# The tail of a two-layer cross-attention kernel: another order of its last block, one inverse root less, and the last products moved from GpSimd to VectorE

## The chip, the cores and the metric

The kernel runs on one core of a Trainium2 chip. A core has five engines, each with its own instruction stream: TensorE (PE) multiplies matrices and writes to the accumulator memory (`ps`), ScalarE (ACT) applies functions element by element, VectorE (DVE) does element-wise arithmetic and reductions, GpSimd (POOL) does element-wise arithmetic too, and SyncE (SP) issues transfers. Engines wait for each other through semaphores. The metric is the device time of one launch in microseconds (us); lower is better.

## The reference

Input `x` is [2, 1024, 256], the context [2, 77, 256], all float32. Layer 0 is self-attention, cross-attention and a gated feed-forward network, each behind a layer norm and with a residual. Layer 1 is one cross-attention with a single head and an RMS norm at the end. The change touches layer 1 alone:

```python
Q = x @ Wq.T + bq;  K = ctx @ Wk.T + bk;  V = ctx @ Wv.T + bv
attn = softmax(Q @ K.T / sqrt(256), axis=-1)
out  = attn @ V @ Wfc.T + bfc
y    = out + x
return norm_w * (y * rsqrt(mean(y * y, axis=-1) + 1e-8))
```

## The kernel before

The 2048 rows of `x` are 16 tiles of 128 rows, and 4 blocks (`blk` 0 to 3) of 4 tiles (`TPB`); blocks 0 and 1 belong to the first batch element. `x` stays in SBUF, [128, 16, 256], and each step adds its result to it. The order on each engine is written out by hand: the five functions `_(eng)` at the end of `build` are the five instruction streams.

Layer 1's matrices are folded ahead into `g1`, `cb` and `vw`, so that a block needs these steps:

- `turn` and `turn_copy` (X3): `x` is turned by TensorE, and ScalarE copies it to `xT`;
- `l1_scores`: 8 matmuls against `g1`; `l1_max` (VectorE): adds `cb`, takes the row maximum, scales it;
- `l1_exps` (ScalarE): 4 exponentials of 128x77 with their sums;
- `l1_turn` (TensorE): turns the 4 tiles of exponentials; `l1_turn_copy` (ScalarE): copies them to `p1T`;
- `l1_weigh` (TensorE): 4 products with `vw`, one per tile, each written to its own bank; a block's product may overwrite a bank once the residual of the block before has read it (`l_y`);
- `l1_residual` (VectorE): a reciprocal of the sums, then 4 multiply-adds of 128x256 into `x`;
- `l1_squares` (ScalarE): 4 squares of 128x256 with their sums (`l_sq`);
- `l1_root` (VectorE): the inverse root in 12 chained instructions, 3 to start and 3 Newton steps of 3, each of which waits for the one before;
- the end: y times the root times `norm_w`. For blocks 0 to 2 ScalarE multiplies by the root (`l1_scale`) and GpSimd by `norm_w` (line 664, 4 products of 128x256 a block); for block 3 VectorE does both in one instruction (line 1888). SyncE then stores the block (line 569), 512 KB.

The scores of blocks 0 to 2 are made while the feed-forward network still runs; block 3 alone has its scores after it. What follows the network is called the tail here. Its order stands at lines 1198 to 1208 (TensorE), 1459 to 1473 (ScalarE) and 1875 to 1889 (VectorE). Line numbers in the text are those of this kernel.

Of the kernel before, what the change touches and what calls it, by code (L numbers as in the profile page):

```python
# [33 lines left out]
ALU = mybir.AluOpType  # L34
# [3 lines left out]
B, S, D = 2, 1024, 256  # L38
# [4 lines left out]
BLOCKS = T // BLK  # L43
TPB = BLK // P
# [26 lines left out]
RMS_EPS = 1e-8  # L71
# [11 lines left out]
ROW_BO1, ROW_BO2, ROW_BFF2, ROW_W, ROW_BFC = range(5)  # L83


def build(nc, a):
    with ExitStack() as ctx:
        ends, sizes = {}, {}

        def sb(name, shape, dt=F32):  # L90
            t = ctx.enter_context(nc.sbuf_tensor(name, shape, dt))
            ends[name] = nc.sbuf_base
            sizes[name] = int(np.prod(shape[1:])) * mybir.dt.size(dt)
            return t
# [5 lines left out]
        def sem(name):  # L100
            return ctx.enter_context(nc.semaphore(name))

        def scratch(name, shape, dt):
# [10 lines left out]
        x = sb("x", [P, TILES, D])  # L114
# [11 lines left out]
        rows = sb("rows", [P, 5, D])  # L126
# [63 lines left out]
        m1, nm1, sum1, r1, ss1, rms, ms, half_ms = (sb(n, [P, BLOCKS, TPB]) for n in ("m1", "nm1", "sum1", "r1", "ss1", "rms", "ms", "half_ms"))  # L190
# [49 lines left out]
        l_full, l_added, l_max, l_exp, l_turned, l_pT, l_pv, l_y, l_sq, l_root, l_scaled, l_out, l_last = (  # L240
            sem(f"l_{n}") for n in ("full", "added", "max", "exp", "turned", "pT", "pv", "y", "sq", "root", "scaled", "out", "last"))
# [163 lines left out]
        def _(eng):  # L405
# [155 lines left out]


            out_v = a["out"].rearrange("b (t p) d -> p (b t) d", p=P)
            for blk in range(BLOCKS):
                if blk < BLOCKS - 1:
                    eng.wait_ge(l_out, TPB * (blk + 1))
                else:
                    eng.wait_ge(l_last, TPB)
                eng.dma_start(out_v[:, TPB * blk:TPB * blk + TPB, :], x[:, TPB * blk:TPB * blk + TPB, :]).then_inc(y_out, 16)
            eng.wait_ge(y_out, 16 * BLOCKS)  # L570

# [4 lines left out]
        def _(eng):  # L576
# [81 lines left out]
                        eng.tensor_tensor(lo, m.rearrange("p (t n) -> p t n", t=HT), hi, ALU.subtract).then_inc(m_parts, 1)  # L658


            for blk in range(BLOCKS - 1):
                for i in range(TPB * blk, TPB * blk + TPB):
                    eng.wait_ge(l_scaled, i + 1)
                    eng.tensor_tensor(x[:, i, :], x[:, i, :], rows[:, ROW_W, :], ALU.mult).then_inc(l_out, 1)


        @block.tensor
        def _(eng):
# [486 lines left out]
            def l1_turn(blk):  # L1155
                eng.wait_ge(l_exp, TPB * (blk + 1))
                if blk >= 2:
                    eng.wait_ge(l_pT, blk - 1)
                for t in range(TPB):
                    mm_ = eng.transpose(ps[0:CTX, LINEAR + blk % 2, P * t:P * t + P], s1[:, blk, t, :], ident[:, :])  # L1160
                mm_.then_inc(l_turned, 1)

            def l1_weigh(blk):
                eng.wait_ge(l_pT, blk + 1)
                for t in range(TPB):
                    n = TPB * blk + t
                    if blk >= 1:
                        eng.wait_ge(l_y, n - TPB + 1)
                    eng.matmul(ps[:, WIDE[t], 0:D], p1T[0:CTXP, blk, P * t:P * t + P],
                               vw[0:CTXP, blk // 2, :], start=True, stop=True).then_inc(l_pv, 1)  # L1170
# [4 lines left out]
            for n in range(FC * BLOCKS + FF_LAG):  # L1175
# [14 lines left out]
                blk, i = x3_step(n)  # L1190
# [6 lines left out]
            last = BLOCKS - 1  # L1197
# [5 lines left out]
            l1_scores(last)  # L1203
            l1_turn(2)
            l1_weigh(1)
            l1_weigh(2)
            l1_turn(last)
            l1_weigh(last)


# [1 line left out]
        def _(eng):  # L1212
            def turn_copy(phase, blk):

                for c in range(NC):
                    eng.wait_ge(turn_full, 2 * TURNS.index((phase, blk)) + c + 1)
                    src = ps[:, turn_bank(phase, blk, c), :]
                    if phase in (ATT1, ATT2):
                        eng.activation(attT[blk % 2][:, c, :], src, ACT.Copy).then_inc(turn_done, 1)
                    elif phase == X3:  # L1220
                        eng.activation(xT[:, c, BLK * blk:BLK * blk + BLK], src, ACT.Copy).then_inc(turn_done, 1)
                    else:
                        i = COL_LN + 4 * (LN1, LN2, LN3).index(phase)
                        eng.activation(xT[:, c, BLK * blk:BLK * blk + BLK], src, ACT.Identity,
                                       scale=cols[:, i + c:i + c + 1], bias=cols[:, i + 2 + c:i + 3 + c]).then_inc(turn_done, 1)
# [186 lines left out]
            for n in range(FC * BLOCKS):  # L1412
                blk, f = divmod(n, FC)
# [3 lines left out]
                i = COL_FF + FC + f  # L1417
# [10 lines left out]
                done, i = x3_step(n)  # L1428
# [5 lines left out]
            def l1_exps(blk):  # L1434
                eng.wait_ge(l_max, 2 * (blk + 1))
                for t in range(TPB):
                    eng.activation(s1[:, blk, t, :], s1[:, blk, t, :], ACT.Exp, scale=L1_SCALE, bias=nm1[:, blk, t:t + 1],
                                   accum_out=sum1[:, blk, t:t + 1]).then_inc(l_exp, 1)

            def l1_turn_copy(blk):  # L1440
                eng.wait_ge(l_turned, blk + 1)
                eng.activation(p1T[0:CTX, blk, :], ps[0:CTX, LINEAR + blk % 2, :], ACT.Copy).then_inc(l_pT, 1)

            def l1_squares(blk):
                for t in range(TPB):
                    n = TPB * blk + t
                    eng.wait_ge(l_y, n + 1)
                    if n >= 1:
                        eng.wait_ge(l_sq, n)
                    eng.activation(sq[:, :], x[:, n, :], ACT.Square, accum_out=ss1[:, blk, t:t + 1]).then_inc(l_sq, 1)  # L1450

            def l1_scale(blk):
                eng.wait_ge(l_root, blk + 1)
                for t in range(TPB):
                    y = x[:, TPB * blk + t, :]
                    eng.activation(y, y, ACT.Copy, scale=rms[:, blk, t:t + 1]).then_inc(l_scaled, 1)

            last = BLOCKS - 1
# [2 lines left out]
            l1_turn_copy(0)  # L1461
            l1_turn_copy(1)
            turn_copy(X3, last)
            l1_turn_copy(2)
            l1_squares(0)
            l1_exps(last)
            l1_squares(1)
            l1_turn_copy(last)
            l1_scale(0)
            l1_squares(2)  # L1470
            l1_scale(1)
            l1_squares(last)
            l1_scale(2)


        @block.vector
        def _(eng):
# [23 lines left out]
            def root_steps(v, y, w, h, scale, e, ready=None):  # L1501


                for out, ops in ((w, (v, scale, e, ALU.mult, ALU.add)), (h, (w, -0.5, None, ALU.mult)),
                                 (y.bitcast(I32), (w.bitcast(I32), -0.5, float(0x5F3759DF), ALU.mult, ALU.add))):
                    at = begin(eng.tensor_scalar(out, *ops))
                    yield
                    eng.wait_ge(dve_step, at)
                for i in range(3):
                    for in0, in1 in ((y, y), (w, h)):  # L1510
                        at = begin(eng.tensor_tensor(w, in0, in1, ALU.mult))
                        yield
                        eng.wait_ge(dve_step, at)
                    ins = eng.scalar_tensor_tensor(out=y, in0=w, scalar=1.5, in1=y, op0=ALU.add, op1=ALU.mult)
                    if i == 2 and ready is not None:
                        ins.then_inc(ready, 1)
                        return
                    at = begin(ins)
                    yield
                    eng.wait_ge(dve_step, at)  # L1520
# [325 lines left out]
                    eng.scalar_tensor_tensor(out=x[:, n, :], in0=ps[:, WIDE[t], 0:D], scalar=r1[:, blk, t:t + 1],  # L1846
                                             in1=x[:, n, :], op0=ALU.mult, op1=ALU.add).then_inc(l_y, 1)

            def l1_root(blk):
                eng.wait_ge(l_sq, TPB * (blk + 1))  # L1850
                for _ in root_steps(ss1[:, blk, :], rms[:, blk, :], ms[:, blk, :], half_ms[:, blk, :], 1.0 / D, RMS_EPS, l_root):
                    pass

            last_piece, after_cross = after_cross, chain(1, 1)
            for n in range(FC * BLOCKS + FF_LAG):
# [8 lines left out]
                blk, f = divmod(n, FC)  # L1864
                if f == 4 and blk + 1 < BLOCKS:
                    x_low(blk + 1)
                blk, f = divmod(n - FF_LAG, FC)
# [3 lines left out]
                blk, i = x3_step(n)  # L1871
# [3 lines left out]
            last = BLOCKS - 1  # L1875
            l1_residual(0)
            l1_max(last)
            l1_residual(1)
            l1_root(0)
            l1_residual(2)  # L1880
            l1_root(1)
            l1_residual(last)
            l1_root(2)
            l1_root(last)
            eng.wait_ge(l_root, BLOCKS)
            for t in range(TPB):
                y = x[:, TPB * last + t, :]
                eng.scalar_tensor_tensor(out=y, in0=y, scalar=rms[:, last, t:t + 1],
                                         in1=rows[:, ROW_W, :], op0=ALU.mult, op1=ALU.mult).then_inc(l_last, 1)


# ---- launch: one core; the host only lays data out
# [40 lines left out]
```

## Time and profile before

| | |
|---|---|
| median of 3 runs | 755.87 us (753.74, 755.87, 755.88) |
| the profiled execution's own time | 756.13 us |
| its span, first to last instruction | 753.9 us |
| mean granted TensorE clock | 0.949 of full speed |
| last product on VectorE starts | 748.83 us |

The profile is of one execution. Times in its rows are us from the start of the span. A row of the timeline has the start, the duration, the engine, the source line, the operation, what it writes and reads (buffer names without their numbers; the exponentials' array shows as `probs`), the shapes and the count; in brackets the idle time before it and who ended that. A row may merge several instructions of one kind. A matrix product of float32 shows as two MATMUL records.

### The profile page before, as it was taken

To read this page: it belongs to the slowest core of one execution; us is meant where nothing else is said; L and a number is where in the kernel's file an instruction comes from. 1 tells how busy PE (TensorE), PEld (TensorE's weight loads), DVE (VectorE), ACT (ScalarE), POOL (GpSimd) and SP (SyncE) were. 2 spreads that over 40 slices of the span, in tenths; PEclk is the share of its full clock that TensorE was granted. 3 is DMA by queue.
4 is the path that set the end of the run, shared out by engine and by line. 5 is a ranking of instruction groups with operands and counts; after the bars stand their busy time and mean duration, and the time that the engine had idled before them with its cause. 6 is when DMAs were issued, how large, how long until landed. Compare 5 with 4: busy or idle time off the path is not lost.

```text
span 753.9 us, 11161 instructions
## 1 busy us (share of the span) xinstructions
PE 669.6 (89%) x4072; PEld 320.7 (43%) x4072; DVE 538.1 (71%) x929; ACT 488.4 (65%) x853; POOL 99.0 (13%) x152
## 2 busy tenths in 40 slices
PE   4989799999999999999999879679989999999982
PEld 2644122222222222222223335325547878888871
DVE  6678989999999999999974527636853854343367
ACT  2543289999999999999998643446553233233374
POOL 2081800000000000000000100264100110000004
PEclk9999699999999999999999987878998999999995
DMA  9457440202020200000000021111000000000003
GB/s 297 182 190 232 104 181 1 71 1 71 1 72 1 53 19 5 25 2 29 2 1 1 33 78 33 48 56 42 3 1 1 0 1 1 1 1 1 1 0 112
DMA packets 35113, 36.87 MB, mean 49 GB/s; under 512 B 6132, under 2 KB 28276, under 8 KB 34804
## 3 DMA queue, kind: packets, MB, share of 16 engines
q1 hardware_dynamic: 33904, 35.87, 14.9%
q0 software_dynamic: 1024, 0.24, 0.3%
q8 instruction: 32, 0.52, 0.3%
q14 instruction: 21, 0.17, 0.1%
q10 hardware_dynamic: 132, 0.07, 0.0%
HBM read 23.09 MB, written 12.74 MB: 48 GB/s over the span
## 4 chain that ended last, share of the span: by engine, by line
PE 65%; DVE 17%; ACT 10%; issue 5%; DMA 1%; POOL 1%; SPq 0%; ACTq 0%; DVEq 0%; POOLq 0%
PE ps L935 15%; PE ps L923 10%; DVE mm L1559 7%; PE ps L719 6%; ACT probs L1318 6%; PE ps L1121 4%; PE ps L1122 4%; PE ps L1123 4%; PE ps L752 3%; PE ps L896 3%; PE ps L705 2%; PE ps L1038 2%; PE ps L727 2%; PE ps L1137 2%; PE ps L1136 2%
## 5 line engine op out<-in xcount | busy, mean ns | idle before, releaser
L1318 ACT ACTIVATE probs<-ps,unfit 128x512 f32<-128x512 f32 x512 | 311.5, 691 | 30.0 <-PE ps L923 25.3
L1559 DVE TENSOR_REDUCE mm<-ps 128x2 f32<-128x1024 f32 x256 | 299.5, 1219 | 14.8 <-PE ps L752 10.9
L923 PE MATMUL ps<-stack 50*128 50x512 f16 x512 | 147.7, 390 | 6.9 <-ACT probs L1318 0.7
L935 PE MATMUL ps<-probs,v 128*32 128x512 f32 x1024 | 138.9, 615 | 2.7 <-ACT outT L1323 2.7
L752 PE MATMUL ps<-stack 48*128 48x512 f16 x512 | 109.1, 392 | 12.7 <-DVE mm L1559 6.6
L923 PEld LDWEIGHTS ps<-stack 50*128 50x128 f16 x512 | 37.0, 93 | 174.1 <-ACT probs L1318 165.1
L1418 ACT ACTIVATE early<-ps,cols 128x512 f32<-128x512 f32 x32 | 22.0, 688 | 91.9 <-PE ps L1123 91.9
L1820 DVE SCALAR_TENSOR_TENSOR hid<-ps,cols,early 128x512 f32<-128x512 f32 x32 | 24.0, 750 | 76.1 <-PE ps L1123 76.1
L612 POOL TENSOR_TENSOR x<-x,rows 128x512 f32<-128x512 f32 x24 | 31.7, 1333 | 165.3 <-DVE tok L1537 165.2
L1373 ACT ACTIVATE probs<-ps,unfit 96x1024 f32<-96x1024 f32 x32 | 35.5, 1109 | 26.6 <-PE ps L1029 26.5
L1121 PE MATMUL ps<-x_hi,wff_hi 128*128 128x512 f32 x128 | 52.3, 408 | 0.0
L1122 PE MATMUL ps<-x_lo,wff_hi 128*128 128x512 f32 x128 | 51.0, 398 | 0.0
L1123 PE MATMUL ps<-x_hi,wff_lo 128*128 128x512 f32 x128 | 50.9, 398 | 0.0
L752 PEld LDWEIGHTS ps<-stack 48*128 48x128 f16 x512 | 26.2, 94 | 54.6 <-DVE mm L1559 30.6
L654 POOL TENSOR_SCALAR mu<-mm 128x16 f32<-128x16 f32 x13 | 3.3, 253 | 287.4 <-DVE mm L1575 287.4
L935 PEld LDWEIGHTS ps<-probs,v 128*32 128x32 f32 x1024 | 20.7, 108 | 41.4 <-issue 30.9
L705 PE MATMUL ps<-ident,tok 128*128 128x128 f32 x160 | 25.5, 300 | 14.2 <-DVE tok L1537 9.6
L896 PE MATMUL ps<-wo,wkv 128*128 128x256 f32 x128 | 36.3, 418 | 1.8 <-DVE x L1654 1.1
L1761 DVE TENSOR_REDUCE mm<-ps 128x8 f32<-128x616 f32 x32 | 25.3, 791 | 16.7 <-PE ps L1018 16.5
L1136 PE MATMUL ps<-wff_hi,hid_hi 128*128 128x256 f32 x128 | 36.5, 285 | 0.0
L1137 PE MATMUL ps<-wff_lo,hid_hi 128*128 128x256 f32 x128 | 36.1, 282 | 0.0
L1138 PE MATMUL ps<-wff_hi,hid_lo 128*128 128x256 f32 x128 | 35.8, 279 | 0.0
(168 smaller groups left out, 871.6 us busy)
## 6 DMA issues: line engine op xcount, KB each, us to landing
v_groups<-early SPq DMA_DIRECT2D x8, 512.0 KB, 3.1
stack<-q_parts SPq DMA_DIRECT2D x64, 64.0 KB, 2.0
v<-v_groups SPq DMA_DIRECT2D x8, 512.0 KB, 4.0
x<-in_x SPq DMA_DIRECT2D x4, 512.0 KB, 7.7
q_parts<-probs SPq DMA_DIRECT2D x8, 256.0 KB, 3.8
k_parts<-probs SPq DMA_DIRECT2D x8, 256.0 KB, 2.2
stack<-k_parts SPq DMA_DIRECT2D x16, 128.0 KB, 2.6
stack<-q_parts SPq DMA_DIRECT2D x64, 32.0 KB, 1.8
```

Of the source, the lines that this page charges most:

```text
L719: mm_ = eng.matmul(ps[:, proj_bank(u), 0:n], w[:, c, P * o:P * o + P], src[:, c, c0:c0 + n], start=(c == 0), stop=(c == NC - 1))
L752: mm_ = eng.matmul(ps[:, 2 * s_slot(G, j, i) + tile, :], qs[rows_i, slot, half, q, P * t:P * t + P], stack[rows_i, SLOTS + slot, q, BLK * ...
L896: mm_ = eng.matmul(ps[:, out_bank(k), 0:D], attT[i // TPB][:, c, P * t:P * t + P], w[:, c, :], start=(c == 0), stop=(c == NC - 1))
L923: eng.matmul(ps[:, st_bank(n), :], stack[rows_of(tile, KROWS), SLOTS + slot, q, P * kc:P * kc + P], qs[rows_of(tile, KROWS), slot, half, q ...
L935: mm_ = eng.matmul(ps[32 * h:32 * h + 32, PV, :], v1[:, G % 2, kc, 32 * h:32 * h + 32], probs[:, k % 2, h, :], start=(kc == 0), stop=(kc = ...
L1121: eng.matmul(ps[:, bank, :], wh, xh[:, c, :], start=(c == 0), stop=False)
L1122: eng.matmul(ps[:, bank, :], wh, xl[:, c, :], start=False, stop=False)
L1123: mm_ = eng.matmul(ps[:, bank, :], wl, xh[:, c, :], start=False, stop=(c == NC - 1))
L1136: eng.matmul(out, hh, w2h, start=(f == 0), stop=False)
L1137: eng.matmul(out, hh, w2l, start=False, stop=False)
L1318: eng.activation(probs[:, k % 2, HEADS[h], :], ps[:, st_bank(n), :], ACT.Exp, scale=unfit[:, 0:1]).then_inc(exp_done, 1)
L1559: eng.tensor_reduce(dst, ps[:, 2 * slot:2 * slot + 2, :], AX.X, ALU.max).then_inc(s_red, 1)
```

## The change

On TensorE the transposes of block 3 move ahead of the products of block 2. On ScalarE the squares of block 0 move ahead of the copy of block 2's transposes, the exponentials of block 3 and the copy of its transposes move ahead of the squares of block 1, and the scaling of blocks 1 and 2 goes away. On VectorE the residuals of blocks 2 and 3 follow one another, the inverse roots of blocks 2 and 3 are one chain of 12 instructions on 128x8, and the new function `l1_final` does for blocks 1, 2 and 3 what was done for block 3 alone. GpSimd keeps the products of block 0. SyncE stores in the order 0, 1, 3, 2.

```diff
@@ -561,11 +561,11 @@
 
 
             out_v = a["out"].rearrange("b (t p) d -> p (b t) d", p=P)
-            for blk in range(BLOCKS):
-                if blk < BLOCKS - 1:
-                    eng.wait_ge(l_out, TPB * (blk + 1))
+            for n, blk in enumerate((0, 1, BLOCKS - 1, 2)):
+                if n == 0:
+                    eng.wait_ge(l_out, TPB)
                 else:
-                    eng.wait_ge(l_last, TPB)
+                    eng.wait_ge(l_last, TPB * n)
                 eng.dma_start(out_v[:, TPB * blk:TPB * blk + TPB, :], x[:, TPB * blk:TPB * blk + TPB, :]).then_inc(y_out, 16)
             eng.wait_ge(y_out, 16 * BLOCKS)
 
@@ -658,10 +658,9 @@
                         eng.tensor_tensor(lo, m.rearrange("p (t n) -> p t n", t=HT), hi, ALU.subtract).then_inc(m_parts, 1)
 
 
-            for blk in range(BLOCKS - 1):
-                for i in range(TPB * blk, TPB * blk + TPB):
-                    eng.wait_ge(l_scaled, i + 1)
-                    eng.tensor_tensor(x[:, i, :], x[:, i, :], rows[:, ROW_W, :], ALU.mult).then_inc(l_out, 1)
+            for i in range(TPB):
+                eng.wait_ge(l_scaled, i + 1)
+                eng.tensor_tensor(x[:, i, :], x[:, i, :], rows[:, ROW_W, :], ALU.mult).then_inc(l_out, 1)
 
 
         @block.tensor
@@ -1203,8 +1202,8 @@
             l1_scores(last)
             l1_turn(2)
             l1_weigh(1)
+            l1_turn(last)
             l1_weigh(2)
-            l1_turn(last)
             l1_weigh(last)
 
 
@@ -1461,16 +1460,14 @@
             l1_turn_copy(0)
             l1_turn_copy(1)
             turn_copy(X3, last)
+            l1_squares(0)
             l1_turn_copy(2)
-            l1_squares(0)
             l1_exps(last)
+            l1_turn_copy(last)
             l1_squares(1)
-            l1_turn_copy(last)
             l1_scale(0)
             l1_squares(2)
-            l1_scale(1)
             l1_squares(last)
-            l1_scale(2)
 
 
         @block.vector
@@ -1846,10 +1843,17 @@
                     eng.scalar_tensor_tensor(out=x[:, n, :], in0=ps[:, WIDE[t], 0:D], scalar=r1[:, blk, t:t + 1],
                                              in1=x[:, n, :], op0=ALU.mult, op1=ALU.add).then_inc(l_y, 1)
 
-            def l1_root(blk):
-                eng.wait_ge(l_sq, TPB * (blk + 1))
-                for _ in root_steps(ss1[:, blk, :], rms[:, blk, :], ms[:, blk, :], half_ms[:, blk, :], 1.0 / D, RMS_EPS, l_root):
+            def l1_root(first, end):
+                eng.wait_ge(l_sq, TPB * end)
+                for _ in root_steps(*(v[:, first:end, :] for v in (ss1, rms, ms, half_ms)), 1.0 / D, RMS_EPS, l_root):
                     pass
+
+            def l1_final(blk, roots):
+                eng.wait_ge(l_root, roots)
+                for t in range(TPB):
+                    y = x[:, TPB * blk + t, :]
+                    eng.scalar_tensor_tensor(out=y, in0=y, scalar=rms[:, blk, t:t + 1],
+                                             in1=rows[:, ROW_W, :], op0=ALU.mult, op1=ALU.mult).then_inc(l_last, 1)
 
             last_piece, after_cross = after_cross, chain(1, 1)
             for n in range(FC * BLOCKS + FF_LAG):
@@ -1876,17 +1880,14 @@
             l1_residual(0)
             l1_max(last)
             l1_residual(1)
-            l1_root(0)
+            l1_root(0, 1)
             l1_residual(2)
-            l1_root(1)
             l1_residual(last)
-            l1_root(2)
-            l1_root(last)
-            eng.wait_ge(l_root, BLOCKS)
-            for t in range(TPB):
-                y = x[:, TPB * last + t, :]
-                eng.scalar_tensor_tensor(out=y, in0=y, scalar=rms[:, last, t:t + 1],
-                                         in1=rows[:, ROW_W, :], op0=ALU.mult, op1=ALU.mult).then_inc(l_last, 1)
+            l1_root(1, 2)
+            l1_final(1, 2)
+            l1_root(2, BLOCKS)
+            l1_final(last, 3)
+            l1_final(2, 3)
 
 
 # ---- launch: one core; the host only lays data out
```

ScalarE's stream from the first exponentials of the tail to its end; `probs` with `nm1` are exponentials, `p1T` the copy of the transposes, `sq` the squares, `x<-x,rms` the scaling. Before:

```order
L1437 ACTIVATE probs,sum1<-probs,nm1 128x77 x12
L1442 ACTIVATE p1T<-ps 77x512 x2
L1221 ACTIVATE xT<-ps 128x512 x2
L1442 ACTIVATE p1T<-ps 77x512
L1450 ACTIVATE sq,ss1<-x 128x256 x4
L1437 ACTIVATE probs,sum1<-probs,nm1 128x77 x4
L1450 ACTIVATE sq,ss1<-x 128x256 x4
L1442 ACTIVATE p1T<-ps 77x512
L1456 ACTIVATE x<-x,rms 128x256 x4
L1450 ACTIVATE sq,ss1<-x 128x256 x4
L1456 ACTIVATE x<-x,rms 128x256 x4
```

After:

```order
L1436 ACTIVATE probs,sum1<-probs,nm1 128x77 x12
L1441 ACTIVATE p1T<-ps 77x512 x2
L1220 ACTIVATE xT<-ps 128x512 x2
L1449 ACTIVATE sq,ss1<-x 128x256 x4
L1441 ACTIVATE p1T<-ps 77x512
L1436 ACTIVATE probs,sum1<-probs,nm1 128x77 x4
L1441 ACTIVATE p1T<-ps 77x512
L1449 ACTIVATE sq,ss1<-x 128x256 x4
L1455 ACTIVATE x<-x,rms 128x256 x4
L1449 ACTIVATE sq,ss1<-x 128x256 x8
```

The last copy to `p1T`, block 3's, stands two places earlier, and one scaling group is left of three (the third of before follows the rows shown).

TensorE's stream from the products of block 0 to its end; L1160 and L1159 are the transposes of the exponentials, L1169 and L1168 the products with `vw`. Before:

```order
L1169 MATMUL ps<-vw,p1T 128x256 x4
L1151 MATMUL ps<-g1,xT 128x77 x8
L1160 MATMUL ps<-ident,probs 77x128 x4
L1169 MATMUL ps<-vw,p1T 128x256 x8
L1160 MATMUL ps<-ident,probs 77x128 x4
L1169 MATMUL ps<-vw,p1T 128x256 x4
```

After:

```order
L1168 MATMUL ps<-vw,p1T 128x256 x4
L1150 MATMUL ps<-g1,xT 128x77 x8
L1159 MATMUL ps<-ident,probs 77x128 x4
L1168 MATMUL ps<-vw,p1T 128x256 x4
L1159 MATMUL ps<-ident,probs 77x128 x4
L1168 MATMUL ps<-vw,p1T 128x256 x8
```

Block 3's four transposes stand between the products of blocks 1 and 2; the products of blocks 2 and 3 follow one another.

VectorE's stream from the residual of block 2 on. Before, where a root of 12 instructions (its first five shown) stands ahead of the next residual:

```order
L1842 RECIPROCAL r1<-sum1 128x4
L1846 SCALAR_TENSOR_TENSOR x<-ps,r1,x 128x256 x4
L1506 TENSOR_SCALAR ms<-ss1 128x4
L1506 TENSOR_SCALAR half_ms<-ms 128x4
L1506 TENSOR_SCALAR rms<-ms 128x4
L1511 TENSOR_TENSOR ms<-rms 128x4
L1511 TENSOR_TENSOR ms<-ms,half_ms 128x4
```

After:

```order
L1839 RECIPROCAL r1<-sum1 128x4
L1843 SCALAR_TENSOR_TENSOR x<-ps,r1,x 128x256 x4
L1839 RECIPROCAL r1<-sum1 128x4
L1843 SCALAR_TENSOR_TENSOR x<-ps,r1,x 128x256 x4
L1503 TENSOR_SCALAR ms<-ss1 128x4
```

The residual of block 3 follows that of block 2 with no root between; behind the rows of after come block 1's root, its 4 final products, the root on 128x8 and 8 final products.

## Rows read from the trace of the kernel before

**Rows 1.** Chain of waits, a piece from the tail: start, us, engine, what.

```profile
748.83 0.48 DVE x L1888
```

**Rows 2.** Timeline of VectorE in the tail: start, us, line, operation, shapes, count.

```profile
724.91 1.71 DVE L1846 SCALAR_TENSOR_TENSOR x<-ps,r,x 128x256 f32<-128x256 f32 x4 [2.19 <-PE ps L1169]
...
728.90 0.17 DVE L1838 TENSOR_SCALAR nm<-m 128x4 f32<-128x4 f32 x1
...
729.18 1.66 DVE L1846 SCALAR_TENSOR_TENSOR x<-ps,r,x 128x256 f32<-128x256 f32 x4
731.14 0.17 DVE L1506 TENSOR_SCALAR ms<-ss 128x4 f32<-128x4 f32 x1 [0.30 <-ACT sq L1450]
...
733.40 0.17 DVE L1842 RECIPROCAL r<-sum 128x4 f32<-128x4 f32 x1
...
735.18 0.16 DVE L1506 TENSOR_SCALAR ms<-ss 128x4 f32<-128x4 f32 x1
...
737.10 0.65 DVE L1514 SCALAR_TENSOR_TENSOR rms<-ms,rms 128x4 f32<-128x4 f32 x1
...
739.33 0.17 DVE L1842 RECIPROCAL r<-sum 128x4 f32<-128x4 f32 x1
...
741.11 0.36 DVE L1506 TENSOR_SCALAR ms<-ss 128x4 f32<-128x4 f32 x1
...
744.51 0.16 DVE L1506 TENSOR_SCALAR ms<-ss 128x4 f32<-128x4 f32 x1
...
748.83 1.67 DVE L1888 SCALAR_TENSOR_TENSOR x<-x,rms,rows 128x256 f32<-128x256 f32 x4
```

**Rows 3.** Timeline of GpSimd in the tail.

```profile
735.63 2.78 POOL L664 TENSOR_TENSOR x<-x,rows 128x256 f32<-128x256 f32 x4 [127.11 <-ACT x L1456]
740.03 2.78 POOL L664 TENSOR_TENSOR x<-x,rows 128x256 f32<-128x256 f32 x4 [1.62 <-ACT x L1456]
745.21 2.77 POOL L664 TENSOR_TENSOR x<-x,rows 128x256 f32<-128x256 f32 x4 [2.41 <-ACT x L1456]
```

**Rows 4.** Lines 1846 and 664: ns of one (min/median/max), first and last start.

```profile
L1846 DVE SCALAR_TENSOR_TENSOR x<-ps,r,x x16: 473/474/484, 724.9 to 740.7; 128x256 f32<-128x256 f32 x16
...
L664 POOL TENSOR_TENSOR x<-x,rows x12: 722/726/727, 735.6 to 747.3; 128x256 f32<-128x256 f32 x12
```

**Rows 5.** Timeline of ScalarE in the tail.

```profile
724.37 1.06 ACT L1221 ACTIVATE xT<-ps 128x512 f32<-128x512 f32 x2
...
731.01 0.34 ACT L1437 ACTIVATE probs<-probs,nm 128x77 f32<-128x77 f32 x1
...
732.38 0.40 ACT L1450 ACTIVATE sq<-x 128x256 f32<-128x256 f32 x1
...
734.58 0.57 ACT L1442 ACTIVATE p1T<-ps 77x512 f32<-77x512 f32 x1
735.05 1.69 ACT L1456 ACTIVATE x<-x,rms 128x256 f32<-128x256 f32 x4
736.65 0.40 ACT L1450 ACTIVATE sq<-x 128x256 f32<-128x256 f32 x1
```

**Rows 6.** Timeline of TensorE in the tail.

```profile
724.13 1.97 PE L1169 MATMUL ps<-vw,p1T 96*128 96x256 f32 x8 [0.21 <-ACT p1T L1442]
...
728.12 3.66 PE L1169 MATMUL ps<-vw,p1T 96*128 96x256 f32 x16
732.52 0.66 PE L1160 MATMUL ps<-ident,probs 128*77 128x128 f32 x4 [0.75 <-ACT probs L1437]
735.20 3.78 PE L1169 MATMUL ps<-vw,p1T 96*128 96x256 f32 x8 [2.02 <-ACT p1T L1442]
```

**Rows 7.** Busy time in two stretches: stretch, us, busy per engine (count), PEclk, DMA share, GB/s.

```profile
734.20:735.10 0.90, 0.00 (x0) 0.00 (x0) 0.90 (x3) 0.90 (x4) 0.00 (x0) 1.00 0.00 0
735.20:736.00 0.80, 0.80 (x2) 0.71 (x3) 0.70 (x5) 0.80 (x3) 0.37 (x1) 0.50 0.00 0
```

**Rows 8.** Transfers, 747.9 to 753.9 us in 40 slices: busy share, tenths.

```profile
DMA  0000001999999999810000029999999997000000
```

## The prediction

> **What bounds the kernel now.** The change begins after the feed-forward network, so I read only the tail, in four views. First the chain of waits, which ends with VectorE's final products at 748.83 [rows 1]. Then VectorE's timeline: the root of block 0 waits 0.30 for ScalarE's squares, and from then on no row has a wait [rows 2]. From 731.14 to the end of the last product at 750.50 there are 19.36 us without a pause: root of block 0 2.26 (731.14 to 733.40), residual of block 2 1.78 (to 735.18), root of block 1 4.15 (to 739.33), residual of block 3 1.78 (to 741.11), roots of blocks 2 and 3 3.40 and 4.32 (to 748.83), final products of block 3 1.67. Four roots of the same 12 instructions take 2.26, 4.15, 3.40 and 4.32, so 5.09 us over three times 2.26 need a cause. GpSimd's timeline gives it: its three groups of products run 735.63 to 738.41, 740.03 to 742.81 and 745.21 to 747.98 [rows 3], and inside them a root's instruction takes 0.65 in place of 0.17 [rows 2], nearly the 0.73 of one GpSimd product [rows 4]. Held VectorE instructions step with GpSimd's products. The residual's multiply-add, which reads `ps` and `x`, is not held: its 16 instances lie between 473 and 484 ns [rows 4], though the residual between 739.33 and 741.11 ran into the second group. Last the transfers: each 512 KB store moves data for 1.7 us, beginning 0.8 us after its block is done [rows 8], and the span ends at 753.9, which is 3.40 after the last product.
>
> **The change part by part.** On ScalarE, squares of block 0 can begin when the last copy to `xT` is over, at 725.43 (724.37 plus 1.06) [rows 5], and follow the residual of 724.91 to 726.62 [rows 2]. Four take 2.20 (732.38 to 734.58) [rows 5]. They are done about 727.9, before block 2's copy can start at 728.3, so this move costs nothing. Root of block 0 then waits for VectorE alone, which leaves the residual of block 1 at 730.8 (729.18 plus 1.66) [rows 2] instead of 731.14: 0.3 gained.
>
> Block 3's maximum is ready at 729.07 (728.90 plus 0.17) [rows 2]. Its exponentials, 1.37 for the four (731.01 to 732.38) [rows 5], run from 729.1 to about 730.6 instead of 731.0 to 732.5. TensorE, whose products of block 1 are half of the 16 in 3.66 from 728.12 [rows 6] and end at 729.95, does the transposes from 730.6 to 731.3 (0.66) [rows 6], then the products of block 2 from 731.3 to 733.1. These are later than before, and what hides that is VectorE, which is in block 0's root until 733.1. ScalarE copies block 3's transposes from 731.3 to 731.8 (0.47, 734.58 to 735.05) [rows 5], so they are waiting 3 us earlier than before.
>
> VectorE from 730.8, if nothing else ends last: root 0 2.26, to 733.06. Residual 2 1.78, to 734.84. Block 3's products may overwrite a bank when residual 2 has read it, the first at 733.7. At full clock a tile takes 0.46, and the result can be used 0.78 after the start (724.13 to 724.91) [rows 2, 6]: 734.5 for the first, 735.9 for the fourth. Residual 3 wants them at 735.05 and 736.3, so it doesn't wait: 1.78, to 736.62. Root 1 needs the squares of block 1, which ScalarE makes from 731.8 to 734.0, long before. It costs 2.26 plus what GpSimd holds. ScalarE scales block 0 from 734.0 to 735.6 (1.60) [rows 5], GpSimd follows 0.58 behind (735.05 to 735.63) [rows 3, 5], thus 734.55 to 737.33. Most of that lies on the residual, which is not held; root 1 meets what is left, 0.7 us, in which it would have done three instructions and does one or two. The bounds are 0 (GpSimd done or VectorE first) and 0.9 (two instructions of 0.65 for two of 0.2); I take 0.4, nearer to the first as only one whole product is left. Root 1 ends at 739.28.
>
> The Trainium skill, "SBUF — State Buffer", section "Who interferes with whom", says that VectorE and GpSimd share a port pair as an exclusive lock for a whole instruction, that a VectorE instruction with two SBUF inputs competes for it when GpSimd reads SBUF, and that the one that starts first wins. The rows bear out the hold, step by step. By that rule root 1 loses at most the one product still under way, 0.73, and the time would be 0.3 above mine. It also speaks against the new final products, which read `x` and `norm_w` both from SBUF; no row here shows a large VectorE instruction of that kind beside GpSimd.
>
> Final products of block 1: four at 0.40, 1.60 (the 1.67 of 748.83 holds the last one's drain) [rows 2], to 740.88; they begin 1.9 us after GpSimd's end. The joined root needs all of ScalarE's squares: after the scaling, block 2 to 737.8 and block 3 to 740.1 (2.20 each and 0.1 for the last sum). The cover is 0.8 us; if ScalarE were later than that, each us is a us on the path. A root on eight columns is in no row; a final product on 256 columns costs 0.2 us more than a root's instruction on four [rows 2], so twelve instructions on eight cost between 0 and 2.4 more. By proportion to the columns it is 0.004 each, and I take 0.05 in all, as eight lie next to four: 2.31, to 743.19. Block 3's final products to 744.79, block 2's to 746.46 (1.60 and 1.67).
>
> The sum: one root less (2.26), the holds of three groups less (5.09), the earlier start 0.3, together 7.65; against it eight more final products 3.20, the hold 0.4 and 0.05: 4.0 less, and the last product ends at 746.46 instead of 750.50. Blocks 1 to 3 lose ScalarE's scaling and GpSimd's products as well, which were beside the path. SyncE issues blocks 0, 1, 3, 2; each wait is for the block that VectorE finishes next, so none queues behind a late one. The last two stores are 1.67 apart and each moves data for 1.7 with the engines full in all slices between [rows 8]: between 0 and, if the second had to wait for the whole 3.40 of the first, 1.7; I take 0.1, as the rows show the data phase alone and not the whole time occupying the engines. The profiled execution becomes 756.13 less 3.9, the median of the runs shown 755.87 less 3.9: 752.0 us.
>
> **The rivals.** TensorE's clock. It is granted at full speed until 735.1 and at half (1.2 instead of 2.4 GHz) from 735.2 [rows 7], after an idle 0.75, transposes of 0.66 and an idle 2.02; the eight records of block 3 then take 3.78 instead of 1.83 [rows 6]. In the new order the idle pieces ahead of those products are about 0.65 and 0.6 with 2.5 us of work between, so I expect full speed. If it falls at block 3's products all the same, the last tile is ready about 737.8, residual 3 ends at 738.3 (1.65 later), GpSimd's hold is gone (0.4), and the time is 753.2. If block 2's products are slow too, 3.78 from 731.3 and 3.78 from 735.05, residual 3 ends at 739.5: 754.5, within what can't be told from no change.
>
> GpSimd's products come later. If ScalarE reaches the scaling of block 0 some 1.5 us or more later than 734.0, all four products lie on root 1, which then costs what root 1 costs now, 4.15: 1.9 in place of 0.4, 753.5. For it speaks that the scaling stands behind block 3's copy and block 1's squares; against it that none of these waits for anything late.
>
> The other side: TensorE at half speed already from block 1's products at 728.12. These end at 731.9, the transposes (twice 0.66) at 733.2, block 2's products at 737.0, block 3's at 740.8, one behind the other because the change puts all on one stretch. Residual 3 ends at 741.5, then 2.26, 1.60, 2.31 and 3.27 give 750.94, past the 750.50 of now; with the stores 756.4, slower than before. It decides from a fall before 728.1. Against it: TensorE's work is unchanged to 729.95, and the clock now holds 7 us past that point.
>
> The change doesn't do what it says if the holds don't come from GpSimd but go with the roots: then 5.09 stay but for one root's share of 1.7, the gain is 0.9 and the time 755.0. Against it, root 0 has no hold and three groups of holds begin and end with GpSimd's.
>
> **How the numbers follow.** Forecast 752.0: 0.74. Late GpSimd, 753.5: 0.08. Half clock at block 3, 753.2: 0.08; at blocks 2 and 3, 754.5: 0.04. Half clock from block 1, 756.4: 0.02. Holds that stay, 755.0: 0.04. The forecast's own range comes from the hold (0.4 less to 0.5 more) and the stores (0.1 less to 0.4 more): 751.4 to 753.0. The same kernel's runs lie between 753.74 and 755.88, and a median of few can fall 2 us lower, so the low end is 749.8; the high end, 754.0, takes in the late GpSimd and the first clock case. A measurement can tell about 0.3%, 2.3 us, from no change: faster means below 753.6. The forecast gives 0.70 of its 0.74 to faster, the two cases near 753.4 about 0.11 of 0.16; with the scatter 0.81 faster, 0.16 the same, 0.03 slower.
>
> **What would show it.** In the new profile: a root of block 0 from 730.8; transposes of block 3 near 730.6; the two last residuals back to back without a wait for TensorE; a granted clock of 1.00 under block 3's products; one GpSimd group only, 734.5 to 737.3, with at most two held VectorE instructions; three roots of about 2.3; final products of 0.40 each; the joined root waiting for nothing; the last product ending near 746.5 and the span 3.4 or 3.5 later. Wrong would be a wait of the joined root for the squares, held instructions in the final products, or residual 3 waiting for TensorE.

## The result, and the profile after

The changed kernel takes 749.96 us (median of 20 runs, 745.85 to 752.70) against 753.87 us for the kernel before (20 runs, 747.73 to 756.65). The ratio is 0.9943, 95% interval [0.9926, 0.9961]: faster by 0.57%, or 4.3 us, with 2.9 to 5.6 in the interval; the two medians are 3.9 us apart. The forecast was 3.9 us less, and 752.0 us, which is 1.9 less than these 753.87. The profiled execution of the changed kernel has a span of 750.1 us against 753.9. Line numbers of the changed kernel are one (TensorE, ScalarE, GpSimd) or three (VectorE) lower than before; the final products are at line 1855.

VectorE's timeline after, the rows that answer to [rows 2]; columns as there:

```profile
730.79 0.16 DVE L1503 TENSOR_SCALAR ms<-ss 128x4 f32<-128x4 f32 x1
...
733.04 0.17 DVE L1839 RECIPROCAL r<-sum 128x4 f32<-128x4 f32 x1
733.25 1.66 DVE L1843 SCALAR_TENSOR_TENSOR x<-ps,r,x 128x256 f32<-128x256 f32 x4
734.83 0.17 DVE L1839 RECIPROCAL r<-sum 128x4 f32<-128x4 f32 x1
735.03 1.66 DVE L1843 SCALAR_TENSOR_TENSOR x<-ps,r,x 128x256 f32<-128x256 f32 x4
736.61 0.16 DVE L1503 TENSOR_SCALAR ms<-ss 128x4 f32<-128x4 f32 x1
736.80 0.64 DVE L1503 TENSOR_SCALAR half_ms<-ms 128x4 f32<-128x4 f32 x1
737.47 0.17 DVE L1503 TENSOR_SCALAR rms<-ms 128x4 int32<-128x4 int32 x1
...
739.45 1.67 DVE L1855 SCALAR_TENSOR_TENSOR x<-x,rms,rows 128x256 f32<-128x256 f32 x4
741.04 0.17 DVE L1503 TENSOR_SCALAR ms<-ss 128x8 f32<-128x8 f32 x1
...
743.46 3.26 DVE L1855 SCALAR_TENSOR_TENSOR x<-x,rms,rows 128x256 f32<-128x256 f32 x8
```

No row has a wait in brackets. The root of block 0 starts at 730.79 and the two residuals follow one another. The root of block 1 has a single held instruction (0.64 at 736.80, where the same instruction of the joined root takes 0.17) and takes 2.84 (736.61 to 739.45). The joined root takes 2.42 on eight columns (741.04 to 743.46). The last product ends at 746.72, where [rows 2] give 750.50.

GpSimd after, and the multiply-add of the residual, which reads `ps` (ns of one as in [rows 4]):

```profile
734.63 2.78 POOL L663 TENSOR_TENSOR x<-x,rows 128x256 f32<-128x256 f32 x4 [126.10 <-ACT x L1455]
```

```profile
L1843 DVE SCALAR_TENSOR_TENSOR x<-ps,r,x x16: 472/476/486, 724.9 to 736.2; 128x256 f32<-128x256 f32 x16
```

One group is left, and the last residual and part of the one before lie inside it without getting longer. ScalarE after, its exponentials, copy and scaling and the last sum of squares:

```profile
729.13 0.36 ACT L1436 ACTIVATE probs<-probs,nm 128x77 f32<-128x77 f32 x1 [0.20 <-DVE nm L1835]
...
731.36 0.59 ACT L1441 ACTIVATE p1T<-ps 77x512 f32<-77x512 f32 x1 [0.75 <-PE ps L1159]
...
734.06 1.69 ACT L1455 ACTIVATE x<-x,rms 128x256 f32<-128x256 f32 x4
...
740.17 0.19 ACT L1449 ACTIVATION_READ_ACCUMULATOR sq<-x 128x1 f32 x1
```

The squares end at 740.36, 0.7 before the joined root wants them. TensorE after, against [rows 6], and its clock under block 3's products, against [rows 7]:

```profile
730.66 0.66 PE L1159 MATMUL ps<-ident,probs 128*77 128x128 f32 x4 [0.62 <-ACT probs L1436]
731.16 1.89 PE L1168 MATMUL ps<-vw,p1T 96*128 96x256 f32 x8
733.88 1.97 PE L1168 MATMUL ps<-vw,p1T 96*128 96x256 f32 x8 [0.83 <-DVE x L1843]
```

```profile
733.90:735.90 2.00, 1.95 (x8) 1.39 (x8) 1.97 (x7) 2.00 (x7) 1.27 (x2) 1.00 0.00 0
```

Block 3's products take 1.97 instead of 3.78, at a granted clock of 1.00. The transfers between 744.1 and 750.1 in 40 slices, against [rows 8]:

```profile
DMA  0000000000000699999999978999999999200000
```

The last two stores now move their data with hardly a pause, and the span ends 3.4 after the last product, as before.

### The profile page after: what moved, and what is told of

Same layout as the page of the kernel before. It is cut to its first block, busy times and chain, and to the rows that moved or that the text cites. A ratio compares the mean times of both kernels' runs of the same rounds, so it can differ in the third digit from the quotient of the medians.

```text
span 750.1 us, 11141 instructions
## 1 busy us (share of the span) xinstructions
PE 668.1 (89%) x4072; PEld 321.1 (43%) x4072; DVE 535.2 (71%) x925; ACT 485.6 (65%) x845; POOL 93.5 (12%) x144
## 4 chain that ended last, share of the span: by engine, by line
PE 65%; DVE 17%; ACT 10%; issue 5%; DMA 1%; POOL 1%; SPq 0%; ACTq 0%; DVEq 0%; POOLq 0%
PE ps L934 15%; PE ps L922 10%; DVE mm L1556 7%; PE ps L718 6%; ACT probs L1317 5%; PE ps L751 4%; PE ps L1120 4%; PE ps L1121 4%; PE ps L1122 4%; PE ps L895 3%; PE ps L704 3%; PE ps L1037 2%; PE ps L726 2%; PE ps L1136 2%; PE ps L1135 2%
```

## The experiments

Runs of one kernel lie up to 10 us apart, while the parts of the change are worth 0.5 to 5. So the measure is the **tail**: from TensorE's first transposes of exponentials to the end of the span, in each kernel's profiled execution. For the last column: in the same series as e1 to e4 the kernel before took 753.77 us (1 run), with e5 to e8 754.01 (25 runs), with e9 to e12 754.24 (21 runs).

| kernel | tail starts | span | tail | time of the runs, us (count) |
|---|---|---|---|---|
| before | 722.01 | 753.9 | 31.9 | 753.87 (20) |
| changed | 722.04 | 750.1 | 28.1 | 749.96 (20) |
| e8, e12: changed again | 720.13, 720.17 | 748.2, 748.2 | 28.1, 28.0 | 750.09 (10), 749.76 (12) |
| e1: old order | 716.25 | 745.5 | 29.3 | 747.36 (1) |
| e2: separate roots | 722.19 | 752.5 | 30.3 | 754.52 (1) |
| e3: old scaling | 722.22 | 752.4 | 30.2 | 754.75 (1) |
| e4: GpSimd beside final products | 722.40 | 752.4 | 30.0 | 754.45 (1) |
| e5: early scaling of block 0 | 721.70 | 749.4 | 27.7 | 749.80 (10) |
| e6, e11: joined kernel | 717.14, 722.60 | 744.3, 749.8 | 27.2, 27.2 | 747.11 (4), 747.59 (10) |
| e7: joined, two Newton steps | 721.67 | 748.7 | 27.0 | 749.35 (10) |
| e9: before, scaling alone | 720.50 | 752.4 | 31.9 | 754.41 (1) |
| e10: before, joined root alone | 722.16 | 754.8 | 32.6 | 756.73 (1) |

**e1, the order of block 3 undone.** TensorE's transposes of block 3 go back behind block 2's products, and on ScalarE:

```diff
+            l1_turn_copy(2)
             l1_squares(0)
-            l1_turn_copy(2)
             l1_exps(last)
-            l1_turn_copy(last)
             l1_squares(1)
+            l1_turn_copy(last)
             l1_scale(0)
```

> The changed kernel with TensorE's and ScalarE's old order for block 3 (transposes behind the products of block 2, squares of block 0 behind the third copy, block 3's copy behind the squares of block 1). The tail, from the first transposes of exponentials to the end, is 31.9 us before and 28.1 us after. Theory A (VectorE's chain sets the end, the order only keeps block 3's products from being late): block 3's products start about 735.2 after a long idle stretch at half clock, VectorE waits for them in the last residual about 3 us, the tail is 30.5 to 31.3. Theory B (the order is beside the path and the whole gain is GpSimd's holds and the root): 28.1 to 28.5.

Between the two: 29.3. TensorE's products, VectorE's last residual, and the clock:

```profile
729.45 2.62 PE L1168 MATMUL ps<-vw,p1T 96*128 96x256 f32 x8 [2.02 <-ACT p1T L1441]
```

```profile
730.26 1.48 DVE L1843 SCALAR_TENSOR_TENSOR x<-ps,r,x 128x256 f32<-128x256 f32 x3 [0.66 <-PE ps L1168]
732.11 0.48 DVE L1843 SCALAR_TENSOR_TENSOR x<-ps,r,x 128x256 f32<-128x256 f32 x1 [0.37 <-PE ps L1168]
```

```profile
729.45:730.60 1.15, 1.15 (x5) 1.04 (x6) 0.49 (x3) 1.15 (x4) 0.72 (x2) 1.00 0.00 0
...
730.80:732.00 1.20, 1.20 (x4) 0.46 (x2) 0.82 (x2) 1.11 (x5) 1.20 (x3) 0.50 0.00 0
```

VectorE waits for TensorE, as theory A has it, but after the same idle 2.02 ahead of the products the clock fell 1.2 us after they began, not as they began [rows 7], so the two waits shown are 1.0 in all. Block 3's residual is 1.3 longer (729.43 to 732.51, against 1.78), block 0's root starts 0.4 later behind the squares, and the hold on block 1's root is gone (2.39 instead of 2.84): together the 1.2 us of the tail. It should be more in an execution where the clock falls at once; no run shows that. VectorE's own order, residual 3 ahead of block 1's root, stays in e1, and no run puts it back alone.

**e2, the joined root undone:** `l1_root(2, 3)` and `l1_root(3, BLOCKS)` in place of `l1_root(2, BLOCKS)`.

> The changed kernel with separate roots for blocks 2 and 3. Theory A: one chain of 12 more on the path, 2.25 us, tail 30.3. Theory B (the joined root hides behind ScalarE's squares, which end last): under 1 us, tail 28.1 to 29.0.

Theory A: 30.3. The last root and the products behind it:

```profile
743.45 0.16 DVE L1503 TENSOR_SCALAR ms<-ss 128x4 f32<-128x4 f32 x1
...
745.83 3.25 DVE L1855 SCALAR_TENSOR_TENSOR x<-x,rms,rows 128x256 f32<-128x256 f32 x8
```

The second chain costs its whole length, 2.38 from 743.45 to 745.83.

**e3, ScalarE and GpSimd scale blocks 0 to 2 again.** VectorE keeps block 3's final products alone, GpSimd loops over 12 tiles, and ScalarE has

```diff
             l1_squares(last)
+            l1_scale(1)
+            l1_scale(2)
```

> The changed kernel with ScalarE and GpSimd scaling blocks 0 to 2 again, ScalarE's two groups behind all squares. Theory A: VectorE does 3.2 us less but GpSimd's second group holds the joined root by some 1.9, and the third group, behind the root and ScalarE's scaling, ends last: about 747.8, so the tail is 29.0 to 29.6; final products of block 3 on VectorE, which read two arrays in SBUF, are held too and step at 0.7 beside GpSimd. Theory B (only short instructions on four columns are held): the final products keep 0.40 each.

The tail is 30.2, above either figure. The final products of block 3, and GpSimd's third group:

```profile
744.85 2.61 DVE L1857 SCALAR_TENSOR_TENSOR x<-x,rms,rows 128x256 f32<-128x256 f32 x4
```

```profile
745.43 3.29 POOL L663 TENSOR_TENSOR x<-x,rows 128x256 f32<-128x256 f32 x4 [1.65 <-ACT x L1455]
```

The mechanism is theory A's, and it acts both ways: the products are held (2.61 for 1.67), and they hold GpSimd (3.29 for 2.78), which I had left out. SyncE keeps the changed store order here, and the span ends 3.7 after GpSimd's last product (748.72 to 752.4).

**e4, GpSimd beside large final products.**

```diff
+            eng.wait_ge(l_root, 2)
+            for i in range(TPB):
+                eng.tensor_tensor(tok[:, i, :], rows[:, ROW_BO1, :], rows[:, ROW_W, :], ALU.mult)
```

> The changed kernel with four more products on GpSimd, written to an array that nothing reads, released by block 1's root (739.4), so that they lie beside block 1's final products. Theory A (a VectorE instruction with two SBUF inputs waits for each GpSimd product): the four final products take 0.7 each, 2.8 in all, and the tail is 1.1 to 1.3 longer, 29.3. Theory B (only short instructions are held): the four keep 0.40, the first instructions of the joined root take 0.65 instead, and the tail is about 1 us longer all the same; the rows tell the two apart.

Theory A, with a higher price: 1.9 us of tail instead of 1.2. VectorE and GpSimd beside one another, and the ns of one for both lines:

```profile
739.81 3.64 DVE L1858 SCALAR_TENSOR_TENSOR x<-x,rms,rows 128x256 f32<-128x256 f32 x4
```

```profile
739.86 3.31 POOL L666 TENSOR_TENSOR tok<-rows 128x256 f32<-128x256 f32 x4 [2.08 <-DVE rms L1514]
```

```profile
L1858 DVE SCALAR_TENSOR_TENSOR x<-x,rms,rows x12: 480/480/1050, 739.8 to 748.6; 128x256 f32<-128x256 f32 x12
```

```profile
L666 POOL TENSOR_TENSOR tok<-rows x4: 723/899/907, 739.9 to 742.3; 128x256 f32<-128x256 f32 x4
```

The two take turns: four products in 3.56 (739.81 to the next instruction at 743.37), 0.89 each, more than GpSimd's own 0.69 and twice VectorE's 0.40. It is less than 1.09, which the two would need one behind the other (0.40 plus 0.69), so a part of each still overlaps.

**e5, the last hold taken away.** On ScalarE `l1_squares` gets bounds:

```diff
-            l1_squares(1)
+            l1_squares(1, 0, 2)
             l1_scale(0)
+            l1_squares(1, 2)
```

> The changed kernel with ScalarE's scaling of block 0 between the second and the third square of block 1, so that GpSimd's products (733.7 to 736.4) lie wholly beside the residuals of blocks 2 and 3. Theory A (what reads the accumulators and one array in SBUF is not held; only what is left of GpSimd's last product holds block 1's root): no held instruction, the root 2.25 instead of 2.8, tail 27.5 to 27.7 against 28.1. Theory B (the residuals pay once more products lie on them): residuals longer than 1.66 and tail 28.0 or more.

Theory A: 27.7, and block 1's root is whole:

```profile
736.26 0.16 DVE L1504 TENSOR_SCALAR ms<-ss 128x4 f32<-128x4 f32 x1
736.46 0.17 DVE L1504 TENSOR_SCALAR half_ms<-ms 128x4 f32<-128x4 f32 x1
...
738.63 1.67 DVE L1856 SCALAR_TENSOR_TENSOR x<-x,rms,rows 128x256 f32<-128x256 f32 x4
```

2.37 in place of 2.84, although GpSimd's whole group (from 733.41) lies on the two residuals. The gain of 0.4 is read from the profiles: the timed runs (ratio 0.9942 to the kernel before, against 0.9943) don't tell this kernel from the changed one.

**e6 and e11, the joined kernel: VectorE makes all final products.** GpSimd's loop and `l1_scale(0)` go, the stores wait for `l_last` alone, one square of block 1 goes ahead of block 3's copy, and on VectorE

```diff
             l1_residual(last)
-            l1_root(1, 2)
-            l1_final(1, 2)
-            l1_root(2, BLOCKS)
-            l1_final(last, 3)
-            l1_final(2, 3)
+            l1_final(0, 1)
+            l1_root(1, BLOCKS)
+            l1_final(1, 2)
+            l1_final(last, 2)
+            l1_final(2, 2)
```

> The changed kernel without GpSimd in the tail: VectorE makes block 0's final products too, while ScalarE's squares end; one root chain on 128x12 for blocks 1 to 3; one square of block 1 in ScalarE's gap ahead of block 3's copy. Theory A (VectorE's instruction count sets the end): against the changed kernel four final products more (1.6), one root less (2.4) and the hold (0.5) gone: tail 26.8 to 27.4, some 0.8 to 1.2 us less. Theory B (ScalarE's squares or the stores set the end): the joined root waits over 1 us, or the stores queue, and the tail is 28.0 or more.

> The joined kernel (all blocks scaled by VectorE, one root chain for blocks 1 to 3, no GpSimd in the tail) once more, with more runs. Theory A: tail 27.1 to 27.2 again, last product 23.8 after the tail's start, so 0.9 less than the changed kernel: a ratio to before near 0.9935 where the changed kernel has 0.9943. Theory B (the 747.1 of four runs was more than the tail shows): ratio near 0.991.

Theory A in both: 27.2. The joined root waits 0.25 for the squares (e6):

```profile
733.62 0.17 DVE L1496 TENSOR_SCALAR ms<-ss 128x12 f32<-128x12 f32 x1 [0.25 <-ACT sq L1442]
...
736.09 4.84 DVE L1848 SCALAR_TENSOR_TENSOR x<-x,rms,rows 128x256 f32<-128x256 f32 x12
```

The ratios to before are 0.9914 [0.9879, 0.9948] and 0.9929 [0.9898, 0.9960]. The tail is 0.9 shorter than the changed kernel's in every profile of the two; the timed intervals overlap with its 0.9943, so the runs alone don't tell them apart.

**e7, two Newton steps** in both chains of the joined kernel (`newton=2`).

> As the joined kernel (all blocks on VectorE, one root chain for blocks 1 to 3), and each of its two root chains has two Newton steps, 9 instructions in place of 12, so the root is less exact. Theory A: 0.6 less on each chain, the first of which may be eaten by the wait for the squares: tail 26.0 to 26.7. Theory B (squares end last): no less than the joined kernel with three steps.

Neither: 27.0. VectorE's last product comes 23.0 after the tail's start against 23.8 in e6, so VectorE's part is as theory A has it, with part of the saving eaten by a longer wait for the squares:

```profile
738.02 0.17 DVE L1496 TENSOR_SCALAR ms<-ss 128x12 f32<-128x12 f32 x1 [0.71 <-ACT sq L1442]
```

But the span ends 4.0 after the last product, not 3.4, although the stores follow one another at 1.6 us as in e6. The transfers of the last 6 us have, in e7 alone of the 14 profiles, one packet of another queue:

```profile
q14 instruction: 1, 0.01, 0.6%
```

That packet, 8 KB of instructions, starts at 746.22 and takes 0.55. Most of the last store is over by 747.3, and a rest trickles on at 20 to 27 GB/s, against some 270 to 380 before: its last 40 packets end within 0.7 us of one another, in e6 within 0.15. So the instruction packet is the likely cause of the late 0.6, which no run tests; without it the tail would be near 26.4 (an estimate), inside theory A's range.

**e8 and e12, the changed kernel again.**

> The changed kernel once more. The question is the scatter: runs of the same kernel lay 10 us apart. Theory A (the scatter comes from the stages ahead of the tail, with TensorE's clock): the tail is 28.0 to 28.2 again, whatever the span, and the tail's start moves between 716 and 722.5. Theory B (the tail scatters too): the tail differs by over 0.5.

> The changed kernel a third time, on the same chip as the joined one. Theory A: tail 28.0 to 28.1, some 0.9 above the joined kernel's, and a ratio to before of 0.994 to 0.996. Theory B (scatter in the tail): tail off by over 0.3.

Theory A: 28.1 and 28.0, with ratios to before of 0.9941 and 0.9937, the second just below the 0.994 expected. Over the executions profiled the tail starts anywhere from 716.25 to 722.60, and for one kernel it is the same to 0.1.

**e9, the kernel before with the scaling on VectorE alone:** the changed GpSimd, SyncE and `l1_final`, with separate roots and the old order.

> The kernel before with one part of the change: VectorE makes the final products of blocks 1 to 3, behind all roots; GpSimd keeps block 0; order and four separate roots stay. Theory A: the holds of GpSimd's second and third group (1.14 and 2.06) go, eight final products (3.2) come: nothing gained, tail 31.7 to 32.2 against 31.9. Theory B (the scaling on VectorE is what makes the changed kernel faster): tail 30.5 or less.

Theory A: 31.9, exactly what the kernel before has. VectorE's 12 final products:

```profile
744.13 4.83 DVE L1855 SCALAR_TENSOR_TENSOR x<-x,rms,rows 128x256 f32<-128x256 f32 x12
```

**e10, the kernel before with the joined root alone:** `l1_root(2, BLOCKS)` for the last two of four roots.

> The kernel before with one part of the change: one root chain for blocks 2 and 3; GpSimd keeps three groups. Theory A: the joined root waits for ScalarE's squares of block 3, which stand behind a scaling (743.4 in the old clock of the trace), and GpSimd's third group, now beside block 3's final products, ends last near 749.5: tail 30.7 to 31.3. Theory B (a root less is 2.25 less wherever it stands): 29.4 to 29.8.

Neither: slower than before, 32.6. VectorE and GpSimd:

```profile
743.54 0.17 DVE L1506 TENSOR_SCALAR ms<-ss 128x8 f32<-128x8 f32 x1 [2.19 <-ACT sq L1450]
...
745.97 2.61 DVE L1858 SCALAR_TENSOR_TENSOR x<-x,rms,rows 128x256 f32<-128x256 f32 x4
```

```profile
746.55 3.28 POOL L664 TENSOR_TENSOR x<-x,rows 128x256 f32<-128x256 f32 x4 [3.58 <-ACT x L1456]
```

The root waits 2.19 for the squares, as theory A says, and GpSimd ends at 749.83, near the 749.5 expected. What I missed is SyncE: block 3 is done at 748.58, but its store stands behind the wait for block 2, so two stores go out at 749.8 and the span ends 5.0 later. In e3, with the changed store order, it ends 3.7 after GpSimd's last product. The store order alone was not run.

## Where the prediction held, and the step that failed

The step that failed is the last one, the level from which the gain is taken off: "the median of the runs shown 755.87 less 3.9: 752.0 us". Those three are the first of the 20 runs of the kernel before, and two of them are the fifth and sixth slowest. The median of the 20 is 753.87, 2.0 lower (754.01 and 754.24 in two later series), and less 3.9 that is 749.97, where 749.96 was measured. The text had the warning beside it ("a median of few can fall 2 us lower") and used it for the range only, so 752.0 promised 1.9 us less than 753.87, half of the 3.9 that came. That the two figures agree to 0.01 us is luck: the gain itself is known to 2.9 to 5.6.

The mechanism and the 3.9 us held. The steps, against the profile after. Root of block 0 at 730.8: 730.79. Transposes near 730.6: 730.66. Root of block 1 at 736.62: 736.61. GpSimd 734.55 to 737.33: 734.63 to 737.41. Hold 0.4: 0.47 (2.84 against e5's 2.37), one instruction. Joined root 2.31: 2.42. It waits for nothing, with 0.8 to spare: 0.7. Last product 746.46: 746.72. Span 750.0: 750.1. The clock stays at full speed under block 3's products.

The last product came 0.26 later than the sum has it, and 0.22 of that are a term that the sum put at nothing. Its 2.26 for a root was measured on block 0's root, behind which comes a reciprocal that doesn't read the root; after, it starts 0.08 behind the start of the root's last step (732.96 to 733.04). A final product reads the root and starts 0.20 behind it (739.25 to 739.45). So both later roots cost 0.11 more: 2.37 on four columns (e5), 2.42 on eight. The 0.05 for eight columns was right.

The rule of the Trainium skill ("SBUF — State Buffer", section "Who interferes with whom") bounded the hold at 0.73, and 0.47 is inside. What it says of two SBUF inputs, which no row of before could show, e3 and e4 bear out in the main: such products and GpSimd's hold each other up. A lock for a whole instruction would make about 1.09 for a pair in e4 (an estimate: 0.40 plus 0.69), where 0.89 was measured; the measurement decides. The instruction held at 736.80 reads one tensor only, so the case of two inputs, as the prediction has it, is not the whole of it.

The experiments put a size to each part. Taken from the changed kernel the joined root is worth 2.2 (e2) and the scaling 2.1 (e3); the order is worth 1.2 in one execution (e1). They don't add up to 3.8, because what one brings depends on the others: alone on the kernel before, the scaling brings 0.0 (e9) and the joined root costs 0.7 (e10). The prediction's sum is a sum over VectorE's stream as a whole, and as such it holds. By the rows, the last product ends 3.78 earlier: 0.35 from the start of block 0's root, 1.31 from block 1's root (4.15 to 2.84), 5.30 from the last two roots (7.72 to 2.42), less 3.18 for eight products more. Of the "holds of three groups less (5.09)", about 3.2 belong to the second and third group, and that is just what e9 trades for the eight products.

The rivals. TensorE at half clock under block 3's products, or under the later part of them, does happen when the order is not changed (e1, e9, e10), and in no profile with the changed order. The cases of a late GpSimd, of a fall of the clock from block 1's products and of holds that don't come from GpSimd are not seen; e5 excludes the last, since with GpSimd's group moved ahead of block 1's root the hold is gone.

The scatter of the level lies ahead of the tail, as e8 and e12 show, and about 2 us of it can be placed. The changed kernel's first large products, in the execution of the result and in e8:

```profile
13.93 3.75 PE L718 MATMUL ps<-xT,early 128*128 128x512 f32 x4 [0.96 <-ACT xT L1223]
```

```profile
13.96 1.95 PE L718 MATMUL ps<-xT,early 128*128 128x512 f32 x4 [0.96 <-ACT xT L1223]
```

The same four records start at the same time and go at half the pace in the first. By 27 us e8 is 2.2 ahead, and its tail starts 1.9 earlier. Of the 14 profiles, four have the faster pace there (e1, e6, e8, e12), and these are the four whose tails start earliest. Half the pace is what the half clock gives in [rows 6] and [rows 7], but the profile's granted clock reads 1.00 there in both executions, so that this was the clock is not shown. What sets the pace, and the some 3 us more by which e1 and e6 are ahead, stay open.

## What to carry to other kernels

Find the one engine that never pauses on the final stretch and add up its stream, held instructions included; a saving elsewhere is worth nothing until that stream gets shorter, and a single edit can be worth nothing or less until its partners are there. GpSimd's work beside a chain of short VectorE instructions costs VectorE about a GpSimd product for each instruction that is held (0.65 for 0.17); put it beside VectorE work that reads the accumulators, where it cost nothing. For a change of half a per cent in a kernel whose runs scatter by one per cent, forecast the difference and take the level from many runs.

## What the runs showed of the hardware that I had not expected

Two engines that hold each other up can both lose: in e4 a VectorE product came every 0.89 instead of 0.40, and a GpSimd product took 0.90 instead of 0.73, the two taking turns. TensorE's clock fell at the start of the products in one execution [rows 7] and 1.2 us into them in another (e1), after the same idle 2.02. And one 8 KB instruction packet among the last stores went with an end 0.6 us later (e7).
